# Attention scores of four tokens in one TensorE product, with k in a block diagonal, and stage 1 with the context as moving operand

## The reference

```python
def fake_quant(x, s, z):            # q in 0..255
    return (clip(round(x / s + z), 0, 255) - z) * s
x = x + matmul(fake_quant(layernorm(x)), fake_quant(ctx))        # stage 1, per batch of 32 tokens
h = layernorm(x); q, k, v = (h @ w.T + b for each)               # 32 heads of 16
scores = einsum('bshd,bstd->bsht', q, k) / sqrt(16)              # per token: 32 heads x 32 heads
x = x + einsum('bsht,bstd->bshd', softmax(scores), v)
z = (layernorm(x) @ A_w.T) * gate     # 64 experts of rank 8, gate = softmax over the top 16 router scores
x = x + (z @ B_w.T) * 2
```

## Time and profile before

| what | value |
|---|---|
| median of 3 runs | 147.32 us (145.54 to 147.86) |
| profiled execution | 144.67 us |
| its span on the core | 142.9 us |
| TensorE busy | 117.8 us, 82% |
| VectorE busy | 93.5 us, 65% |
| ScalarE busy | 71.2 us, 50% |
| GpSimd busy | 47.1 us, 33% |
| moved by DMA | 24.44 MB |

### The profile page before, as it was taken

The page is one execution under the profiler, slowest core; times in us unless marked ns, Lnnn a source line. Parts: engine busy times, 40 slices in busy tenths (PEclk is TensorE's granted clock), DMA queues, the critical chain, the costliest instruction groups (busy, mean ns, idle before and its releaser), DMA issues.

```text
span 142.9 us, 4282 instructions
## 1 busy us (share of the span) xinstructions
PE 117.8 (82%) x1864; PEld 70.6 (49%) x1864; DVE 93.5 (65%) x189; ACT 71.2 (50%) x87; POOL 47.1 (33%) x61
## 2 busy tenths in 40 slices
PE   0029657992898999989599999999999799899992
PEld 0024343432566447657155445965444376446881
DVE  5740696417579988699582377799347759893512
ACT  0369976559356999038923991372302115411120
POOL 4018225259507553923407575000830000002000
PEclk9999999999999999999999999999999999999999
DMA  2899999999999920079920100000010000000102
GB/s 63 314 421 419 392 406 403 420 403 382 423 420 384 388 81 5 0 310 381 388 108 5 73 2 0 5 5 5 0 73 2 0 5 5 5 0 21 52 5 73
DMA packets 7093, 24.44 MB, mean 171 GB/s; under 512 B 1185, under 2 KB 1441, under 8 KB 5154
## 3 DMA queue, kind: packets, MB, share of 16 engines
q1 hardware_dynamic: 6928, 24.16, 43.3%
q10 hardware_dynamic: 146, 0.01, 0.1%
HBM read 23.11 MB, written 1.05 MB: 169 GB/s over the span
## 4 chain that ended last, share of the span: by engine, by line
PE 55%; DMA 17%; ACT 11%; DVE 8%; issue 5%; POOL 1%; SPq 0%; DVEq 0%; ACTq 0%
PE ps_b L1042 19%; PE ps_a L1042 14%; DMA wv<-in_L_attn_wv_dram 13%; PE ps_att L1111 5%; ACT cu L422 4%; DMA raw<-in_ctx_dram 4%; PE ps L982 3%; PE ps_att L1122 3%; PE ps_att L1145 2%; ACT v_diag L440 2%; PE ps_t L1023 1%; PE ps L1097 1%; DVE v_diag L839 1%; PE ps_b L1164 1%; PE ps_a L1164 1%
## 5 line engine op out<-in xcount | busy, mean ns | idle before, releaser
L422 ACT ACTIVATE cu<-raw,sc_in,sc_recip 128x2048 uint8<-128x2048 f32 x15 | 30.9, 2088 | 6.4 <-DMA raw<-in_ctx_dram 6.3
L336 POOL TENSOR_SCALAR cbf<-cu 128x2048 bf16<-128x2048 uint8 x14 | 26.6, 1903 | 18.6 <-ACT cu L422 16.8
L324 POOL TENSOR_SCALAR var_eps<-mean_var 128x1 f32<-128x1 f32 x12 | 2.7, 223 | 55.8 <-DVE mean_var L583 55.7
L982 PE MATMUL ps<-q1T,cbf 128*128 128x33 bf16 x256 | 7.9, 178 | 4.5 <-POOL cbf L336 2.8
L440 ACT COPY v_diag<-vT 32x512 f32<-32x512 f32 x16 | 10.1, 633 | 2.4 <-DVE vT L704 2.1
L1111 PE MATMUL ps_att<-kT,qT 16*32 16x32 f32 x1024 | 10.5, 193 | 0.9 <-issue 0.7
L982 PEld LDWEIGHTS ps<-q1T,cbf 128*128 128x128 bf16 x256 | 7.3, 96 | 7.3 <-POOL cbf L336 3.5
L447 ACT ACTIVATE probs<-probs 128x512 f32<-128x512 f32 x8 | 5.0, 627 | 11.7 <-DVE probs L712 11.7
L1111 PEld LDWEIGHTS ps_att<-kT,qT 16*32 16x32 f32 x1024 | 9.6, 104 | 1.9 <-issue 1.7
L581 DVE BATCH_NORM_STATS2 stats<-x_sb 128x6 f32<-128x512 f32 x12 | 8.2, 686 | 2.1 <-DMA x_sb<-in_x_dram 1.3
L959 PE MATMUL ps_t<-ident_bf,q 128*128 128x128 bf16 x12 | 1.4, 248 | 10.0 <-DVE q L606 10.0
(11 more groups left out here) (135 smaller groups left out, 222.3 us busy)
## 6 DMA issues: line engine op xcount, KB each, us to landing
raw<-in_ctx_dram SPq DMA_DIRECT2D x15, 1024.0 KB, 10.7
raw<-in_ctx_dram SPq DMA_DIRECT2D x2, 512.0 KB, 11.8
wq<-in_L_attn_wq_dram SPq DMA_DIRECT2D x1, 1024.0 KB, 14.0
wk<-in_L_attn_wk_dram SPq DMA_DIRECT2D x1, 1024.0 KB, 12.4
wv<-in_L_attn_wv_dram SPq DMA_DIRECT2D x1, 1024.0 KB, 19.0
wa<-in_L_ffn_A_w_dram SPq DMA_DIRECT2D x1, 1024.0 KB, 13.1
wb<-in_L_ffn_B_w_dram SPq DMA_DIRECT2D x1, 1024.0 KB, 15.5
out_dram<-x_sb SPq DMA_DIRECT2D x3, 256.0 KB, 2.0
```

The costliest lines, as they stand in the source:

```text
L336: nc.gpsimd.tensor_scalar(cbf[:, n % BF_SLOTS, :, :], cu8[:, n % U8_SLOTS, :], -CENTER, 1.0, ALU.add, ALU.mult).then_inc(sem_ctx_bf_pool, 1)
L422: nc.scalar.activation(cu8[:, n % U8_SLOTS, :], raw[:, n % RAW_SLOTS, :], ACT.Identity, bias=sc_in[:, 3:4], scale=sc_recip[:, 2:3]).then_i ...
L982: last = nc.tensor.matmul(ps1[:, m // 2, col:col + LW], cbf[:, n % BF_SLOTS, c, m * P:(m + 1) * P], q1T[:, t, c, b, :], start=(c == 0), st ...
```

## The change

Three things are changed, and the order of the calls on all five engines with them.

1. The scores. A new tile k_diag (128 x 32 tokens x 4 groups x 32 heads) holds k in a block diagonal: ScalarE's place_k copies k of group b to the columns of group b, four copies of 16 partitions x 1024 values per tile. The zeros beside it are set once, by a memset on VectorE. One product then gives the scores of the i-th tokens of all four groups: 128 rows, 32 stationary columns, 128 moving ones; the column group rotates with i. A tile has 32 such products where it had 128 small ones with their weights. Since the order of tokens in the probabilities changes by this, v's tokens are permuted too: ScalarE makes a second, permuted copy of the transposed h2 (h2T_v), which project_v uses.
2. Stage 1. The context (512 columns) is the moving operand, and the transposed x, or a tile of ones, the stationary one (32 columns). The result isn't transposed any more: transpose_y1 and finish_product are gone, and a product with ones gives the column sums, which VectorE's add_colsum adds to x. In tiles 1 to 3 four batches go to four column groups in turn; in tile 0 the batches come one by one, the last one in two halves.
3. k is projected ahead of q.

The core of the diff:

```diff
+            def place_k(t, b):
+                if b == 0:
+                    act.wait_ge(sem_kT_ready, t + 1)
+                    if t == 0:
+                        act.wait_ge(sem_k_zeros, 1)
+                    if t >= 1:
+                        act.wait_ge(sem_scores_done, 2 * t)
+                rows = slice(Q * b, Q * b + HD)
+                nc.scalar.copy(k_diag[rows, :, b, :], kT[rows, :, :]).then_inc(sem_k_placed, 1)
...
                 nc.scalar.copy(h2T[:, :, :], ps_t1[:, :]).then_inc(sem_h2T_ready, 1)
+                nc.scalar.copy(h2T_v[:, :, :].rearrange("p c (l i b) -> p c l i b", l=BPT, b=BPT),
+                               ps_t1[:, :].rearrange("p (c b i l) -> p c l i b", c=KC, b=BPT, l=BPT)).then_inc(sem_h2T_ready, 1)
...
                 for i in range(S * part, S * (part + 1)):
-                    for j in range(BPT):
-                        rows = slice(Q * j, Q * j + HD)
-                        last = nc.tensor.matmul(ps_att[Q * j:Q * j + H, i, :], qT[rows, i, :], kT[rows, i, :],
-                                                start=True, stop=True)
+                    g = i % BPT
+                    last = nc.tensor.matmul(ps_att[Q * g:Q * (g + 1), i - g:i - g + BPT, :], qT[:, i, :],
+                                            k_diag[:, i, :, :], start=True, stop=True)
...
+            def add_colsum(t):
+                dve.wait_ge(sem_colsum_done, t + 1)
+                dve.wait_ge(sem_x_shifted, t + 1)
+                nc.vector.scalar_tensor_tensor(out=x_sb[:, t, :], in0=ps_colsum[:, :], scalar=sc_terms[:, 0:1],
+                                               in1=x_sb[:, t, :], op0=ALU.mult,
+                                               op1=ALU.add).then_inc(sem_colsum_added, 1)
...
-            def product(t, first=0, end=BPT):
-                    for m in range(KC):
-                        col = (m % 2) * BPT * LW + b * LW
-                        for c in range(KC):
-                            last = nc.tensor.matmul(ps1[:, m // 2, col:col + LW],
-                                                    cbf[:, n % BF_SLOTS, c, m * P:(m + 1) * P],
-                                                    q1T[:, t, c, b, :], start=(c == 0), stop=(c == KC - 1))
+            def product(t, first=0, end=BPT, chunks=range(KC)):
+                for c in chunks:
+                    for b in range(first, end):
+                        last = nc.tensor.matmul(ps_colsum[L * b:L * (b + 1), :], ones_bf[:, :],
+                                                cbf[:, (BPT * t + b) % BF_SLOTS, c, :], start=(c == 0),
+                                                stop=(c == KC - 1))
+                if c == KC - 1 and end == BPT:
+                    last.then_inc(sem_colsum_done, 1)
+                for c in chunks:
+                    for b in range(first, end):
+                        last = nc.tensor.matmul(ps_y1[L * b:L * (b + 1), :], q1T[:, t, c, b, :],
+                                                cbf[:, (BPT * t + b) % BF_SLOTS, c, :], start=(c == 0),
+                                                stop=(c == KC - 1))
...
             norm_stats(x_sb[:, 0, :], 0, 0, sem_ln1_stats, sem_ln1_mean)
+            nc.vector.memset(k_diag[:, :, :, :], 0.0).then_inc(sem_k_zeros, 1)
             norm_1(0)
...
-            keep_clock_up(5)
+            keep_clock_up(3)
```

498 lines of the change are left out of this document (254 added, 244 removed).

## The result

The changed kernel takes 148.27 us in the median of 20 executions (147.33 to 148.98), the kernel before, run beside it, 147.24 (144.32 to 148.84). The ratio is 1.0185 [1.0149, 1.0222]: 1.9% slower. The ratio leaves out disturbed executions, of which the kernel before had more; the quotient of the two medians is only 1.007. The profiled executions say the same: span 145.6 us after, 142.9 before. The forecast had the direction and, by the ratio and the spans, half the size.

The account below looks back on a forecast made before the run. wv's load bounds up to 36.8 us, then TensorE's work. Savings of 3.0 us there against delays from ScalarE's copies and queues left the end +1.3 us: 146.0 profiled, scaled to 148.6 us; range 143.0 to 152.2.

Parts of the forecast that it names:

- TensorE's work: Behind 36.86 us, TensorE's work falls by 3.0 us: shorter scores, no y1 transposes, fewer clock-keeping products, less stage 1's loss.
- The third rival: Scores and stage 1: column groups do not run at once; 35 us on top, near 180 us; chance 0.03.
- the second: Rival on ScalarE: place_k copies dearer than 1.1 us; at 1.27, +3.2 or 150.6 us, 2.2% slower; chance 0.27.
- The rule that was weighed: Scores and stage 1, using all rows, would each pay their weight loads, giving the third rival's sum; forecast held context's trace contradicts it.
- wv absorbs the whole delay: Start: first projection comes at about 28.3 instead of 25.25, but wv still lands at about 36.8; cost nothing, otherwise 3 us.
- the walk: The prediction's step-by-step timing of the engines from the start through the tiles, ending +1.3 us later.
- Both halves end at about 47.0: even: Tile 0's scores, behind project_v(0), end when tile 1's query projection began before, 46.71: no loss.
- let the copies bind the scores: Tile 1: ScalarE free at 57.5, then four copies of 1.1 us; scores(1) start at 61.9 against 58.73, 3.2 us later.
- let the load of context 12 bind v's copies: Tile 1: context 12 lands at 68.3, place_v(1) stands behind its quantisation; context(1) at 74.2 against 71.42, +2.8.
- What is made up: Tiles 1 to 3 recover part of tile 1's 3.2 us: context(1) +2.8, k of tile 3 +2.2, context(3) 124.9 against 123.53.
- under VectorE's cover: Tile 3: router_scores(2) waits for an h3T copy behind the exp, some 1.4 us of idle TensorE, covered by VectorE.
- The first rival: Whole kernel: TensorE alone sets the pace and the new orders fit better; 4.5 us off, 142.7 us, 3.1% faster; chance 0.20.

Follow-up runs that it names:

- the late zeroing: Changed kernel with VectorE's memset of k_diag moved from ahead of norm_1(0) to behind copy_q1T(0): 152.67 us, ratio 1.040 to the kernel before.
- the one attempt in tile 2: Changed kernel with start, context 12 and tile 1 orders altered, plus tile 2's product(3), exp(2,0) and transposed exponentials reordered, h3T early in tile 3: 146.45 us, ratio 1.0024.
- tile 1 mended: Changed kernel with shift_x(2) early, VectorE and ScalarE reordered in tile 1, and h3T's copy ahead of exp(3,0) in tile 3: 144.31 us, ratio 0.9876.
- The short copies of tile 1: Changed kernel with ScalarE's four copies into k_diag cut to one token each in tile 1: 146.97 us, ratio 1.007 to the kernel before.

## Why the prediction was right in its direction and wrong in its size

**Sizes.** Right: a copy of k 1042 ns for 1100, scores 1.89 us for 2.0, product 1.84 for 1.9, the second copy of h2T 0.59 for 0.55, TensorE's work down by 3.15 for 3.0 (2.6 when counted from 36.86, as the forecast has it). The third rival, column groups that don't overlap, is out. So is the second, copies dearer than 1.1 us. The rule that was weighed (the Trainium skill, TensorE: Matmul & The Clock Gate, Part 3: weight loads overlap products only where the row group differs) fails here too: a tile's 64 loads of 110 ns each lie within the 1.89 us of the scores, all 128 rows in each. That the median of 148.27 us lies so near the forecast 148.6 (its sum gives 148.7) is luck: the forecast was scaled from an execution of the kernel before 1.8% below its median, and by ratio and span the loss is twice the one forecast.

**The start.** "wv absorbs the whole delay. Cost: nothing" holds to 0.2 us (37.06 for 36.86), if not in the way described: wv landed at about 35.9, ahead of time, and TensorE's lower clock after its idle 4.3 us used up the rest, 5.33 us for project_k(0). The delay had a second cause, copy_bias(0), that the walk did not name. Nor did it have that the cover is then gone: 2.9 us more reach the end in full, as the late zeroing shows.

**Tile 0.** "Both halves end at about 47.0: even." They ended at 47.30, but both had begun at 45.41, where the first half had begun at 39.19 before. The softmax of the first half lost its six us of lead, ScalarE had only one gap over 0.15 us (0.42, ahead of 43.17) from 40.7 to 57.9 us, and context(0) waited 0.92 us for eT: +1.5, unforeseen. The wait passes through ScalarE's order: VectorE had the second half ready at 50.92, but the exponential came at 54.12, behind v's copies. No run changes this order in tile 0.

**Tile 1.** The times were near (scores at 62.74 for 61.9, context(1) at 74.81 for 74.2), the reasons right only in part. The walk let the copies bind the scores; they ended at 62.45, and TensorE came from product(2), which had waited for context 11, at 62.7. It let the load of context 12 bind v's copies; that was one of three ends within 0.4 us. What remained behind them the walk did not name: VectorE's queue, with the choice of experts ahead of transpose_v(1), and ScalarE's, with the quantisation of context 12 ahead of v's copies whenever its load lands.

**What is made up.** This is the step that failed. It let tiles 2 and 3 give back 1.4 us between context(1) (+2.8) and context(3) (+1.4), and put the end at +1.3. In the trace context(1) is at +3.4, k of tile 3 at +3.2 for +2.2, context(3) at +2.9, the end at +2.7: 0.5 us came back instead of 1.4. TensorE did save its time in tiles 2 and 3, and stood idle for it: 1.09 us for eT in tile 2, 1.59 for h3T in tile 3 (forecast 1.4, "under VectorE's cover"). Of the 1.4 us that the forecast was short, 0.6 stem from context(1), and 0.8, the remainder, from gains of tiles 2 and 3 that other engines' queues held back. The waits are in the trace; that ordering alone could free them is shown for 0.3 us in tile 3, and the one attempt in tile 2 lost time. The first rival, TensorE alone sets the pace (3.1% faster), had the work right and the queues wrong; with tile 1 mended, 1.2% came out.

**Open.** The short copies of tile 1 run 0.9% below the changed kernel in the medians and 0.1 us below it in the one trace; which of its executions is the typical one isn't settled. The trace of the kernel before has a granted clock of 1.00 throughout and that of the changed kernel the dip at its start, so a part of the 2.7 us between them may be one of executions. No run puts the new stage 1 alone into the kernel before, so what it is worth isn't known. Nor is what TensorE waits for after some 214 records of small products.
